# Latents attention: two key products issued ahead of the turned maxima, and four later steps of the key section moved back

## The reference, cut to what matters

```python
x = layer_norm(x, ln_x_w, ln_x_b)                      # 1500 context rows of a batch
latents = layer_norm(latents, ln_l_w, ln_l_b)          # 56 latent rows of a batch
q = latents @ Wq
k, v = split(concat([x, latents]) @ Wkv)               # 1556 rows, 8 heads of 64
q = l2norm(q) * q_scale
k = l2norm(k) * k_scale
sim = where(mask, einsum(q, k) * 8, -max)
attn = softmax(sim)
out = einsum(attn, v) @ Wo
return layer_norm(out, ln_o_w, ln_o_b)
```

## Time and profile before

| What | Value |
| --- | --- |
| median of the runs | 4884.3 us (4883.45 to 4888.38, 3 runs) |
| the profiled execution's own time | 4889.31 us |
| its span in the trace | 4887.5 us |
| busy shares of the span | PE 82%, PEld 51%, DVE 55%, ACT 40%, POOL 20% |
| mean granted clock of TensorE | 0.908 |
| the stage of the change | from the first key product at 3296.1 us to about 4755 us |

### The profile page before, as it was taken

The page is one execution under the profiler, slowest core; times in us unless marked ns, Lnnn a source line. Parts: engine busy times, 40 slices in busy tenths (PEclk is TensorE's granted clock), DMA queues, the critical chain, the costliest instruction groups (busy, mean ns, idle before and its releaser), DMA issues. The chain is left out here.

```text
span 4887.5 us, 95999 instructions
## 1 busy us (share of the span) xinstructions
PE 4009.1 (82%) x39918; PEld 2475.7 (51%) x39918; DVE 2668.6 (55%) x3910; ACT 1968.9 (40%) x3760; POOL 994.9 (20%) x979
## 2 busy tenths in 40 slices
PE   7799588888888896888888884358988988898888
PEld 4544366666666543566666662223444444444444
DVE  3233355555654332566656653337777777777751
ACT  3200144444444000344444452114555555555542
POOL 0000211111111002211111112102333343333330
PEclk8899699999999798899999997669999999999988
DMA  8700355555543001444444430000000000000000
GB/s 234 214 0 0 111 131 133 133 125 129 134 125 71 35 0 48 115 106 106 106 106 106 106 73 5 12 25 13 13 20 20 20 13 20 19 18 15 13 1 21
DMA packets 107980, 329.11 MB, mean 67 GB/s; under 512 B 54151, under 2 KB 55247, under 8 KB 107023
## 3 DMA queue, kind: packets, MB, share of 16 engines
q1 hardware_dynamic: 107567, 323.20, 25.4%
HBM read 168.20 MB, written 7.00 MB: 36 GB/s over the span
## 5 line engine op out<-in xcount | busy, mean ns | idle before, releaser
L1705 POOL TENSOR_TENSOR l_S<-l_S,l_shift 125x448 f32<-125x448 f32 (+1 forms) x416 | 459.3, 1138 | 311.2 <-ACT l_shift L1931 306.3
L1169 ACT ACTIVATE L2a_probs<-ps 125x448 f32<-125x448 f32 x768 | 375.0, 545 | 187.0 <-PE ps L1079 177.0
L1169 ACT ACTIVATE L1a_probs<-ps 125x448 f32<-125x448 f32 x768 | 374.9, 546 | 169.3 <-PE ps L1079 159.4
L1202 DVE TENSOR_REDUCE L1a_chunk_max<-ps 112x1 f32<-112x1000 f32 x256 | 300.5, 1196 | 249.2 <-PE ps L1042 248.7
L1759 PE MATMUL ps<-l_wk,l_xnT 128*125 128x512 f32 (+1 forms) x832 | 426.8, 639 | 2.3 <-ACT l_k_squares L1912 1.7
L1202 DVE TENSOR_REDUCE L2a_chunk_max<-ps 112x1 f32<-112x1000 f32 x256 | 300.6, 1196 | 218.1 <-PE ps L1042 217.7
L1777 PE MATMUL ps<-l_G,l_xnT 128*125 128x448 f32 (+1 forms) x832 | 388.8, 549 | 32.1 <-DVE l_S L2028 32.1
L1912 ACT ACTIVATE l_k_squares<-ps 125x512 f32<-125x512 f32 (+1 forms) x416 | 247.3, 595 | 413.5 <-PE ps L1759 413.5
L2008 DVE TENSOR_REDUCE l_norms<-l_k_squares 125x8 f32<-125x512 f32 (+1 forms) x416 | 278.7, 680 | 232.2 <-ACT l_k_squares L1912 230.2
L1042 PE MATMUL ps<-L1a_keys,L1a_queries 98*112 98x500 f32 x768 | 279.2, 446 | 142.1 <-issue 107.4
L1042 PE MATMUL ps<-L2a_keys,L2a_queries 96*112 96x500 f32 x768 | 279.2, 447 | 109.1 <-issue 73.0
(11 more groups left out here) (381 smaller groups left out, 6947.2 us busy)
## 6 DMA issues: line engine op xcount, KB each, us to landing
L1a_keys<-L1a_k_hi SPq DMA_DIRECT2D x256, 187.5 KB
L2a_keys<-L2a_k_hi SPq DMA_DIRECT2D x256, 187.5 KB
a_ctx_T<-in_ctx_T SPq DMA_DIRECT2D x32, 750.0 KB, 12.0
xn<-L_valid SPq DMA_DIRECT2D x32, 750.0 KB, 7.2
L1a_ctx_T<-in_ctx_T SPq DMA_DIRECT2D x32, 750.0 KB, 5.5
L1a_keys<-L1a_k_lo SPq DMA_DIRECT2D x128, 187.5 KB
L2a_ctx_T<-in_ctx_T SPq DMA_DIRECT2D x32, 750.0 KB, 5.9
L2a_keys<-L2a_k_lo SPq DMA_DIRECT2D x128, 187.5 KB
```

What stands on the lines that cost most here:

```text
L1169: nc.scalar.activation(probs[t % NPR][:, h * HQ // 2:(h + 1) * HQ // 2], s.ps[0:KP, i % 3, 0:HQ // 2], ACT.Exp).then_inc(probs_made, 1)
L1202: ins = nc.vector.tensor_reduce(chunk_max[:, n, 0:1], product, AX.XY, ALU.max)
L1705: nc.gpsimd.tensor_tensor(S[b % 2][0:r, t, :], S[b % 2][0:r, t, :], shift[0:r, :], ALU.add)\
```

## The change

On PE, the products of tiles 0 and 1 of batch b+1 are issued ahead of `turn_maxima(b)`, which stood first. `spread_maxima` moves from behind product 2 to behind product 3, `sums` from 3 to 4, `queries_through_keys` from 5 to 6, `value_product` from 7 to 9, `project_out` from 9 to 12 (the last). In the score section `weigh_latents` moves from ahead of score product 11 to behind score product 12. On ACT, `take_shift` and `take_queries` each move one square back. On DVE, `invert_sums` moves one reduction back, `take_heads` from behind reduction 8 to behind reduction 10, `moments_of` from behind reduction 12 to behind reduction 8, and `take_output` to behind `invert_norms`. No instruction is added or removed, and the waits in the functions stay as they are.

```diff
@@ TensorE
             for b in range(-1, B):
-                if b >= 0:
-                    turn_maxima(b)
                 for t in range(T):
                     if b + 1 < B:
                         key_product(b + 1, t)
-                    if t == 2 and b >= 0:
+                    if t == 1 and b >= 0:
+                        turn_maxima(b)
+                    if t == 3 and b >= 0:
                         spread_maxima(b)
-                    if t == 3 and b >= 1:
+                    if t == 4 and b >= 1:
                         sums(b - 1)
-                    if t == 5 and b + 1 < B:
+                    if t == 6 and b + 1 < B:
                         queries_through_keys(b + 1)
-                    if t == 7 and b >= 1:
+                    if t == 9 and b >= 1:
                         value_product(b - 1)
-                    if t == 9 and b >= 1:
+                    if t == 12 and b >= 1:
                         project_out(b - 1)
                 if b >= 0:
                     weigh(b, 0)
                 for t in range(T):
                     if b >= 0 and t < KT - 1:
                         weigh(b, t + 1)
-                    elif b >= 0 and t == KT - 1:
-                        weigh_latents(b)
                     if b + 1 < B:
                         score_product(b + 1, t)
+                    if b >= 0 and t == KT:
+                        weigh_latents(b)
@@ ScalarE
-                    if t == 3 and b >= 0:
+                    if t == 4 and b >= 0:
                         take_shift(b)
-                    if t == 6 and b + 1 < B:
+                    if t == 7 and b + 1 < B:
                         take_queries(b + 1)
@@ VectorE
                     if b + 1 < B:
                         reduce_squares(b + 1, t)
-                    if t == 4 and b >= 1:
+                    if t == 5 and b >= 1:
                         invert_sums(b - 1)
-                    if t == 8 and b >= 1:
+                    if t == 8 and b >= 0 and b + 2 < B:
+                        moments_of(b + 2)
+                    if t == 10 and b >= 1:
                         take_heads(b - 1)
-                    if t == 11 and b >= 1:
-                        take_output(b - 1)
-                if b >= 0 and b + 2 < B:
-                    moments_of(b + 2)
                 if b + 1 < B:
                     invert_norms(b + 1)
+                if b >= 1:
+                    take_output(b - 1)
                 if b >= 0 and b + 2 < B:
                     invert_std(b + 2)
```

## The result

The changed kernel takes 4955.3 us (median of 4 runs, 4949.7 to 4961.1); the kernel before took 4883.9 beside it (4 runs, 4872.5 to 4888.4). The ratio is 1.015, with a 95% interval of 1.0129 to 1.0171. The forecast was 4837, in a range of 4800 to 4879.

What follows compares the result with a forecast made beforehand. PE was taken to set the pace, losing time to waits and low clock. Gains of 0.0 + 1.1 + 0.45 = 1.55 us a batch, 47 us over 30 turns, with clock cost unchanged, gave 4837 us, range 4800 to 4879.

Steps and rivals of the forecast that it cites:

- walk: Step-by-step timing of one undisturbed batch, from the joined maxima's release of PE, giving a turn of 42.7 us against 44.25.
- product 1: At the turn's start it waits for the turned latents' copy, starts at 0.20 us and delays the turned maxima to 1.1.
- product 4, and the stall ahead of it: In the key section, product 4 waits for square 2 and starts at 4.95 us, leaving PE still for 0.8.
- the projection, and its wait: Behind product 12, PE is ready at 16.15 us but waits 1.05 for the heads, against 0.85 before; projection at 17.2.
- undisturbed turn: One batch's turn without low clock: 42.7 us in place of 44.25, a gain of 1.55.
- Then come the moments on DVE: 2.20 us (70.33 to 72.53): Behind reduction 8, the moved moments take 2.20 us on DVE, the length read at their old place.
- costs nothing: POOL starts about 1 us later, claimed free since its 16.7 us a turn leave 27 free.
- zero difference: Low clock at the turn's start keeps today's cost; bounds were 20 us more gained or 42 us more lost.
- The forecast sum: Key section 0.0, start of scores 1.1, `weigh_latents` move 0.45: 1.55 us a batch, 47 us over 30 turns, 4837 us.
- the stall at the third score product: Its 0.95 us wait for the first scaled tile goes; with the pipeline's fill, 1.1 us is won.
- The moments are fully exposed: Rival, chance 0.11: all 2.20 us of moments delay the first `weigh`, turn 44.9 us, 20 us slower, 4904.
- The rival by which a shorter gap frees the clock: Rival, chance 0.17: a shorter gap at the turn's start removes the half clock, 20 us more gained, 4817 us.

Runs made afterwards that it cites:

- projection's wait filled: Changed kernel plus 14 small unread matmuls ahead of `project_out`: 4891.9 us, ratio 1.0030 to the kernel before.
- one-product variant: Changed kernel with `moments_of` back behind reduction 12 and `turn_maxima` between products 0 and 1: 4796.9 us, ratio 0.9826 to the kernel before.
- short additions: Changed kernel with POOL adding the shift to 8 of 448 columns, so work is left out: 4778.3 us, ratio 0.9793 to the kernel before.
- fills: Changed kernel with POOL's 13 shift additions replaced by equally long memsets of a free tile, scores unshifted: 4804.5 us, ratio 0.9858 to the kernel before.
- moments back: Changed kernel with `moments_of` returned to its old place behind reduction 12: 4832.9 us, ratio 0.9928 to the kernel before.
- latents' step alone: Kernel before with one edit, `weigh_latents` behind score product 12: 4889.4 us, ratio 1.0026.
- moments behind reduction 1: Changed kernel with `moments_of` behind reduction 1, ahead of POOL's additions: 4848.4 us, ratio 0.9955 to the kernel before.
- one product ahead, filled: Changed kernel, `moments_of` behind reduction 12, `turn_maxima` between products 0 and 1, 5 unread matmuls ahead of it: 4784.5 us, ratio 0.9788 to the kernel before.
- before, filled: Kernel before plus 12 small unread matmuls ahead of `turn_maxima`: 4850.2 us, ratio 0.9959.

## Why the prediction was wrong

Its walk, against the changed kernel's turn (us behind the join's release):

| Step | Forecast | Measured |
| --- | --- | --- |
| product 1 | 0.20 | 0.19 |
| turned maxima | 1.1 | 1.16 |
| product 4, and the stall ahead of it | 4.95, 0.8 | 4.99, 0.77 |
| reduction 8 | 12.75 | 12.88 |
| the moments | 2.20 long | 4.94 long |
| the heads | 16.8 | 19.62 |
| the projection, and its wait | 17.2, 1.05 | 20.05, 3.39 |
| first `weigh` | 18.15 | 21.81 |
| undisturbed turn | 42.7 | 45.07 (projection's wait filled) |
| turn as it ran | 42.7, with the clock as today | 47.79 |

**The order on PE was right.** That product 1 waits for the latents' copy and delays the maxima, and that the stall moves to product 4, was found to a tenth of a microsecond. The one-product variant shows its price: 1.1 us a turn (42.99 against 41.87).

**The step that failed** is "Then come the moments on DVE: 2.20 us (70.33 to 72.53)". It took a duration from a place where the last two of POOL's thirteen additions were running and carried it to one where POOL is in the middle of them. These are rows of the kernel before, at the old place:

```profile
4068.82 3.48 POOL L1705 TENSOR_TENSOR l_S<-l_S,l_shift 125x448 f32<-125x448 f32 x3
...
4071.04 0.16 DVE L1986 TENSOR_TENSOR l_moments<-l_stats 125x12 f32<-125x12 f32 x1
...
4071.33 1.00 DVE L1989 TENSOR_SCALAR l_moments<-l_moments 125x12 f32<-125x12 f32 x1
```

The warning stood there: L1985 in the earlier trace rows takes 0.78 us, and L1986, of the same shape, takes 0.16 right behind it. So L1985 is not doing 0.78 us of work. The short additions show the true length, 0.17 each, and the fills show what blocks the instructions with two inputs. The walk said of POOL's later start that it "costs nothing", because it looked at POOL's share of the turn and not at what POOL blocks. The later start is not the main cause: in the kernel before, the same move alone makes the moments 4.0 us long.

**The second failing step is the clock.** It was weighed at the start of a turn alone. With 2.74 us more of moments the projection's wait is 3.39 us, and 1.2 GHz follows it in 29 turns: 2.7 us each, about 80 us in all. The filled wait shows this. At the start of a turn, "zero difference" was too kind as well once the moments are back: with a wait of 1.67 us there (about 2.0 forecast), 23 of 30 turns are longer than 42.99, for a mean of 43.6.

**The sizes add up.** The turn of the kernel with the moments back is 42.99 us undisturbed (forecast 42.7), the moments' blocking makes it 45.07, the low clock 47.79. The forecast sum, without the two, was nearly that experiment's time: 4837 against 4832.9. That is partly luck: the stall at the third score product, which the sum removed (1.1 us), is still there, as L2013 and L2000 are blocked in their turn, and the projection's wait of 1.05, which it kept, is gone. The rest of the walk holds: 42.7 without that wait is 41.65, and the short additions, where no DVE instruction is blocked, have turns of 41.60. One small slip does not matter: from 18.15, PE comes to the third score product at 22.65, not 22.75.

**The rivals.** "The moments are fully exposed" named the right place, at a chance of 0.11. Its price was worked out with the same 2.20 us, so it gave 4904 where 4955 was measured; it had neither the blocking nor the low clock. The rival by which a shorter gap frees the clock fails too. In the changed kernel the start of a turn is free of the low level from the fourth turn on, but the level now falls in the projection's wait. With the moments back, the gap of 1.67 us has it more often than the 3.09 of before.

## What to carry to other kernels

A duration from a trace belongs to its place: where a tiny VectorE instruction ends with GpSimd's current one and is far quicker elsewhere, it is probably held by it, and moving it moves it against another neighbour. Before moving VectorE work with two SBUF inputs or a `tensor_scalar`, lay GpSimd's busy stretches beside the new place. And ask of every new TensorE wait what level the clock has behind it, for the wait's price may nearly double by it, as here: 3.39 us of wait and 2.7 behind it.

## What the runs showed of the hardware that was not expected

**Shorter idle time can mean more low clock.** Turns longer than the undisturbed one by over 0.15 us, among the first 30, against the idle time ahead of PE's restart at the start of a turn:

| Kernel | Idle time, us | Longer turns |
| --- | --- | --- |
| before | 3.09 | 10 |
| latents' step alone | 2.53 | 28 |
| moments back | 1.67 | 23 |
| moments behind reduction 1 | 1.67 | 24 |
| fills in place of additions | 1.67 | 24 |
| short additions | 1.67 | 17 |
| projection's wait filled | 1.67 | 18 |
| one product ahead | 1.48 | 8 |
| one product ahead, filled | 0.41 | 1 |
| before, filled | 0.27 | 0 |

With 0.27 and 0.41 us no turn behind the first is lengthened. From 1.48 to 3.09 us the share does not follow the idle time. The moments' move alone shows it too: its idle time is 3.09 us as in the kernel before, and yet the level is 1.2 GHz behind the start of every turn from the third on. The longer turns come in a pattern (in the kernel before two neighbouring ones in every six, from the seventh turn on), so the length of the turn may have a part in it, but no run shows that. What decides it in a given turn stays open. So an edit that only shortens idle time can be slower by this alone, as the latents' step was.

**Unread matmuls pay.** 12 small matmuls of no use, in idle time of PE, made the kernel before 0.4% faster (0.9945 to 0.9973).
